# The eight normalizations of a two-layer graph network, written out without loops

## The reference, cut to what matters

```
xn = layernorm(x);  x = x + gnn(xn) + mix(xn)          # plain; inside gnn: twice with gain, shift, SiLU;
x  = x + ffn(layernorm(x))                             #        inside mix: once with gain
xn = layernorm(x);  x = x + gnn1(xn) + mix1(xn);  x = x + ffn1(layernorm(x))

layernorm(x):   (x - mean) / sqrt(var + 1e-5)
in gnn:         silu((h - mu) * rsqrt(var + eps) * g + beta)
in mix:         (out - mu) * rsqrt(var + eps) * gamma
```

## Time and profile before

| | us |
|---|---|
| time, median of 3 runs | 5152.3 (5151.81 to 5155.04) |
| the profiled execution's own time | 5157.04 |
| its span in the trace | 5155.4 |
| VectorE busy | 2133.2 (41% of the span) |
| TensorE busy | 3029.4 (59%) |
| the eight normalizations together, first `bn_stats` to last operation | 295.3 |

### The profile page before, as it was taken

One profiled execution on the slowest core, in us unless ns is written; L12 is line 12 of the kernel. 1 busy time (PEld: TensorE's weight loads), 2 busy tenths in 40 slices (PEclk: granted clock), 3 DMA queues, 4 the chain that ended last, 5 costly groups with the idle time before them and its releaser, 6 DMA issues. The chain is left out here.

```text
span 5155.4 us, 68063 instructions
## 1 busy us (share of the span) xinstructions
PE 3029.4 (59%) x14014; PEld 2154.1 (42%) x14015; DVE 2133.2 (41%) x6351; ACT 719.7 (14%) x1795; POOL 1074.6 (21%) x1216
## 2 busy tenths in 40 slices
PE   0577769949949226999287331111000288885998
PEld 0244448838837225777243130000000166663555
DVE  6899940030041640000312543333003888884333
ACT  0011110020022102322011000000000122322222
POOL 1400000000010121000300687777773000000000
PEclk6799989979979658999688665555555688987999
DMA  2511124424410012111234458888664177771000
GB/s 79 201 76 77 75 90 127 127 63 128 127 35 0 0 45 77 49 61 65 61 128 128 149 177 280 280 285 287 220 214 113 39 197 196 195 198 43 13 12 25
DMA packets 487415, 611.30 MB, mean 119 GB/s; under 512 B 78538, under 2 KB 420699, under 8 KB 483643
## 3 DMA queue, kind: packets, MB, share of 16 engines
q1 hardware_dynamic: 372268, 408.37, 25.6%
q0 software_dynamic: 48608, 139.33, 9.0%
q10 hardware_dynamic: 66480, 62.95, 4.3%
HBM read 397.38 MB, written 213.10 MB: 118 GB/s over the span
## 5 line engine op out<-in xcount | busy, mean ns | idle before, releaser
L1850 POOL DMA_INDIRECT srcs_got<-relation_rows,table_row x784 | 802.9, 1024 | 318.6 <-issue 202.2
L2372 PE MATMUL msg_acc<-msg_msg,msg_oh 128*128 128x264 f32 x1666 | 457.4, 439 | 62.8 <-DVE msg_msg L2326 62.5
L477 PE MATMUL counts_acc<-onehot_lo,onehot_key 128*128 128x400 bf16 x1962 | 376.7, 350 | 147.5 <-DVE onehot_lo L459 147.5
L459 DVE TENSOR_SCALAR onehot_lo<-node_ids,source_lo 128x800 bf16<-128x800 int16 x981 | 416.5, 425 | 0.0
L2372 PEld LDWEIGHTS msg_acc<-msg_msg,msg_oh 128*128 128x128 f32 x1666 | 328.1, 211 | 184.0 <-DVE msg_msg L2326 131.6
L1909 PE MATMUL sco_pg<-near_parts,sco_oh 128*128 x1280 | 77.5, 185 | 506.6 <-DVE sco_oh L1928 505.0
L2326 DVE TENSOR_TENSOR msg_msg<-msg_row,scores 128x256 f32<-128x256 f32 x833 | 350.2, 420 | 6.7 <-DMA msg_row<-edge_rows 4.6
L477 PEld LDWEIGHTS counts_acc<-onehot_lo,onehot_key 128*128 128x128 bf16 x1962 | 191.7, 102 | 330.2 <-DVE onehot_lo L459 187.4
L655 PE MATMUL agg_agg<-x_gnn,agg_slab 128*128 128x257 f32 x1250 | 278.0, 382 | 66.9 <-DMA agg_slab<-edge_counts 66.9
L655 PE MATMUL agg_agg<-xn,agg_slab 128*128 128x257 f32 x1250 | 277.2, 381 | 22.9 <-DMA agg_slab<-edge_counts 22.9
L655 PEld LDWEIGHTS agg_agg<-x_gnn,agg_slab 128*128 128x128 f32 x1250 | 238.2, 191 | 102.9 <-DMA agg_slab<-edge_counts 67.3
(11 more groups left out here) (406 smaller groups left out, 4273.5 us busy)
## 6 DMA issues: line engine op xcount, KB each, us to landing
msg_row<-edge_rows SPq DMA_DIRECT2D x833, 128.0 KB, 2.3
edge_rows<-srcs_got SPq DMA_DIRECT2D x112, 927.5 KB, 5.3
agg_slab<-edge_counts SPq DMA_DIRECT2D x50, 1600.0 KB, 8.2
sco_key<-target_keys ACTq DMA_DIRECT2D x256, 160.0 KB
edge_counts<-counts_out SPq DMA_DIRECT2D x100, 400.0 KB, 2.4
relation_rows<-tab_out SPq DMA_DIRECT2D x25, 1060.0 KB, 3.9
wide_w<-L_ffn_W ACTq DMA_DIRECT2D x14, 1024.0 KB, 6.8
srcs_got<-relation_rows,table_row POOLq DMA_INDIRECT x784
```

The source lines that it names most:

```text
L459: ins = nc.vector.tensor_scalar(oh_lo[:, k, j, :], c.nodes[:, 0:LO], lo[:, ds(at + j, 1)], None, ALU.is_equal)
L477: mm = nc.tensor.matmul(acc[:, k, h, 0:HALF_LO], oh_key[:, k, j, :], oh_lo[:, k, j, h * HALF_LO:(h + 1) * HALF_LO], start=False, stop=Fals ...
L1850: nc.gpsimd.indirect_dma_start(got[:, b, j, :], None, rows_of, bass.IndirectOffsetOnAxis(ap=c.row[:, at:at + 1], axis=0)).then_inc(landed[ ...
L2372: nc.tensor.matmul(acc[:, k, 0:D + HD], oh[:, j, :], msg[:, j, :], start=False, stop=False, skip_group_check=True).then_inc(used, 1)
```

## The change

`statistics` and `normalize` become one function with one block, and all its loops are written out:

- the 25 `bn_stats` are 25 instructions; the two sums that don't depend on each other (mean, variance halves) are issued without a wait between them, and the halving of the mean is moved behind the operation that ScalarE's square root waits for;
- plain: VectorE computes `moved` = -mean * rstd (128x25), then 14 tiles as before; the other 11 tiles (ACT_TILES) are ScalarE's, as Identity(x * rstd + moved) with two operands of one value per partition;
- gain: two `scalar_tensor_tensor` per tile in place of three (or two) operations. The first of tile i, (x - mean) * gain into `y`, is issued ahead of the second of tile i - 1, y * rstd + shift. `y` and `z` have four buffers each;
- gain alone (`mixn`): the second operation is y * rstd + residual, written to the residual by VectorE; GpSimd isn't used there. In `gn1` GpSimd still adds.

The diff, cut to its core:

```diff
-def statistics(g, name, src, mean, rstd):
...
-                with v.Fori(0, NT) as i:
-                    nc.vector.bn_stats(st[:, ds(i, 1), :].rearrange("p a s -> p (a s)"),
-                                       tile_of(src, i)).then_inc(loop, 1)
+def normalize(g, name, c, src, dst, gain=None, shift=None, silu=False, add_to=None):
+    deep = 4
...
+        by_act = NT - ACT_TILES if gain is None else NT
+                for i in range(NT):
+                    nc.vector.bn_stats(st[:, i, :], at(src, i)).then_inc(loop, 1)
                 v.wait_ge(loop, NT)
                 link = chain(v, link_s, 0)
+                nc.vector.tensor_tensor(t[:, 2, :], s[2], s[5], ALU.add).then_inc(half, 1)
+                nc.vector.tensor_tensor(mean, s[1], s[4], ALU.add).then_inc(half, 1)
...
+                nc.vector.tensor_scalar(t[:, 1, :], t[:, 2, :], 1.0 / D, EPS, ALU.mult, ALU.add).then_inc(var_s, 1)
+                link(nc.vector.tensor_scalar(mean, mean, 0.5, None, ALU.mult))
                 v.wait_ge(root_s, 1)
+                link(nc.vector.reciprocal(rstd, t[:, 0, :]))
+                if gain is None:
+                    nc.vector.scalar_tensor_tensor(out=moved, in0=mean, scalar=-1.0, in1=rstd,
+                                                   op0=ALU.mult, op1=ALU.mult).then_inc(ready, 1)
+                    for i in range(by_act):
+                        nc.vector.tensor_scalar(at(dst, i), at(src, i), mean[:, i:i + 1], rstd[:, i:i + 1],
+                                                ALU.subtract, ALU.mult).then_inc(last, 1)
+                    return
+                def scale(i):
+                    v.wait_ge(half, i + 3)
+                    if shift is not None:
+                        nc.vector.scalar_tensor_tensor(out=y[:, i % deep, :], in0=y[:, i % deep, :],
+                                                       scalar=rstd[:, i:i + 1], in1=shift,
+                                                       op0=ALU.mult, op1=ALU.add).then_inc(ready, 1)
+                    else:
+                        nc.vector.scalar_tensor_tensor(out=at(add_to, i), in0=y[:, i % deep, :],
+                                                       scalar=rstd[:, i:i + 1], in1=at(add_to, i),
+                                                       op0=ALU.mult, op1=ALU.add).then_inc(ready, 1)
+                for i in range(NT):
+                    if i >= deep:
+                        v.wait_ge(done if silu else ready, i - deep + 1)
+                    nc.vector.scalar_tensor_tensor(out=y[:, i % deep, :], in0=at(src, i), scalar=mean[:, i:i + 1],
+                                                   in1=gain, op0=ALU.subtract, op1=ALU.mult).then_inc(half, 1)
+                    if i:
+                        scale(i - 1)
+                scale(NT - 1)
             @block.scalar
             def _(act):
                 act.wait_ge(var_s, 1)
                 nc.scalar.activation(t[:, 0, :], t[:, 1, :], ACT.Sqrt).then_inc(root_s, 1)
+                if by_act < NT:
+                    act.wait_ge(ready, 1)
+                    for i in range(by_act, NT):
+                        nc.scalar.activation(at(dst, i), at(src, i), ACT.Identity, bias=moved[:, i:i + 1],
+                                             scale=rstd[:, i:i + 1]).then_inc(done, 1)
+                if silu:
+                    for i in range(NT):
                         act.wait_ge(ready, i + 1)
                         if add_to is None:
+                            nc.scalar.activation(at(dst, i), y[:, i % deep, :], ACT.Silu).then_inc(done, 1)
                         else:
+                            if i >= deep:
+                                act.wait_ge(last, i - deep + 1)
+                            nc.scalar.activation(z[:, i % deep, :], y[:, i % deep, :], ACT.Silu).then_inc(done, 1)
+            if silu and add_to is not None:
                 @block.gpsimd
                 def _(pl):
+                    for i in range(NT):
+                        pl.wait_ge(done, i + 1)
+                        nc.gpsimd.tensor_tensor(at(add_to, i), at(add_to, i), z[:, i % deep, :],
                                                 ALU.add).then_inc(last, 1)
```

More of the change, by code:

```diff
@@ L52 @@
 MSPAN = 17
+ACT_TILES = 11
 KSPAN = 5
@@ L524, in statistics, with at @@
         t = g.sb(ctx, f"{name}_tmp", [P, 3, NT])
-        loop, link_s, var_s, root_s = (g.sem(f"{name}_{x}") for x in ("stats", "chain", "var", "root"))
+        mean = g.sb(ctx, f"{name}_mean", [P, NT])
+        rstd = g.sb(ctx, f"{name}_rstd", [P, NT])
+        moved = g.sb(ctx, f"{name}_moved", [P, NT])
+        if gain is not None:
+            y = g.sb(ctx, f"{name}_y", [P, deep, D])
+        if silu and add_to is not None:
+            z = g.sb(ctx, f"{name}_z", [P, deep, D])
+        loop, link_s, var_s, root_s, ready, done, last, half = (
+            g.sem(f"{name}_{x}") for x in ("stats", "chain", "var", "root", "affine", "silu", "written", "half"))
+        def at(x, i):
+            return x[:, i, 0:D]
+        by_act = NT - ACT_TILES if gain is None else NT
         with nc.Block() as block:
@@ L534, in _ @@
                 s = [st[:, :, k] for k in range(6)]
-                link(nc.vector.tensor_tensor(t[:, 0, :], s[1], s[4], ALU.add))
-                link(nc.vector.tensor_scalar(mean, t[:, 0, :], 0.5, None, ALU.mult))
+                nc.vector.tensor_tensor(t[:, 2, :], s[2], s[5], ALU.add).then_inc(half, 1)
+                nc.vector.tensor_tensor(mean, s[1], s[4], ALU.add).then_inc(half, 1)
                 link(nc.vector.tensor_tensor(t[:, 0, :], s[1], s[4], ALU.subtract))
@@ L539, in _ @@
                                                     in1=t[:, 0, :], op0=ALU.mult, op1=ALU.mult))
-                link(nc.vector.tensor_tensor(t[:, 2, :], s[2], s[5], ALU.add))
+                v.wait_ge(half, 2)
                 link(nc.vector.tensor_tensor(t[:, 2, :], t[:, 2, :], t[:, 1, :], ALU.add))
@@ L550, in _ @@
                 nc.scalar.activation(t[:, 0, :], t[:, 1, :], ACT.Sqrt).then_inc(root_s, 1)
[L553 to L599, removed]
@@ L617, in step @@
                                                 ALU.add).then_inc(last, 1)
-                    tiles(pl, NT, step)
 def aggregate(g, name, c, counts, xn, wt, bias, h):
```

2 lines of the change are left out of this document (removed).

## The result

The changed kernel takes 5018.9 us, median of 4 runs (5016.6 to 5025.2), against 5152.1 us (5150.4 to 5155.0) before on the same chip: a ratio of 0.9743, interval 0.9726 to 0.9760. That is 133 us less. In the sessions of `after_sp_pad`, `before_sp_pad`, `three_ops` and `vector_add`, and of `vector_add_again`, `vadd_pool_pad` and `act_tiles10`, every kernel, the one before too (5662 and 5667 us), was slow by some 510 us, nearly all of it between the score stage's first gather and its end, so these times are compared only with times of the same session.

The account below looks back on a forecast made before the run. No engine bounds the whole; VectorE bounds the normalization windows, without filling them. 34 + 27.3 + 21.8 + 10.7 + 13.3 = 107 us off the profiled 5157.0 gives 5050, as a median 5045; 8-in-10 range 5028 to 5080.

Parts of the forecast that it names:

- Statistics: First part of all eight normalizations: unlooped `bn_stats`, no loop setup and a shorter chain save 4.25 us each, 34 us.
- duration less 0.08: Successive VectorE operations overlap, each starting after the previous one's duration less about 0.08 us; 0.344 us for `bn_stats`.
- Plain second parts: Second part of the five plain normalizations: 58.3 us together falls to 5 x 6.2 = 31, ScalarE ending last; gain 27.3 us.
- `gn0` and `mixn`: Their second parts fall from 42.7 and 31.1 us to 20.9 and 20.4; gains 21.8 and 10.7 us.
- gn1: Its second part falls from 50.3 to 37 us, gain 13.3; bounds 6 to 23.
- two things stay: In `gn1`, GpSimd's 7.26 us before its first addition and the mutual exclusion of GpSimd and VectorE were both expected to remain.
- The exclusion of the two engines: In `gn1`, VectorE and GpSimd share a port: 37 us with part running ahead, 44.4 with full durations.
- I put nothing, and 8 either way: Code behind the added instructions shifts, so other loops' turns may change: counted as zero, with 8 us either way.
- No overlap: Rival, 15%: each operation starts only when the one before has ended, giving 5077 us.
- Port: Rival, 10%: VectorE's back-to-back two-input operations give GpSimd the port late; `gn1` stays at 50 us, total 5058.
- Code supply: Rival, 2%: engines wait for about 425 written-out instructions; at 0.3 us of wait each, 5172 us, slower than before.
- Other loops: Rival, 7%: loops kept in other stages land badly, up to 0.23 us more per turn; a hundred turns make 5068 us.

Follow-up runs that it names:

- after_sp_pad: The changed kernel with 12 empty semaphore increments on SP in the block of the fourth plain normalization; 5532.7 us, ratio 0.9776, in a slower session.
- before_sp_pad: The kernel before the change with 48 empty semaphore increments on SP in the block of the fourth plain normalization; 5666.6 us, ratio 1.0007, slower session.
- three_ops: The changed kernel with three written-out operations per tile again in the two normalizations with gain and shift; 5554.2 us, ratio 0.9811, slower session.
- vector_add: The changed kernel with the additions of the second gained normalization on VectorE instead of GpSimd; 5532.3 us, ratio 0.9774, slower session.
- vector_add_again: The same kernel as `vector_add`, run again in another slower session; 5532.6 us, ratio 0.9760.
- vadd_pool_pad: The kernel of `vector_add` with 26 empty semaphore increments on GpSimd in place of its 25 additions and configuration; 5532.5 us, ratio 0.9763, slower session.
- act_tiles10: The changed kernel with 10 in place of 11 plain tiles on ScalarE, nothing else; 5531.8 us, ratio 0.9765, slower session.
- pool_loop: The changed kernel with GpSimd's additions in a loop of 6 turns of 4 again; 5028.2 us beside 5017.5 for the changed kernel, ratio 0.9760.

## Why the prediction was wrong in size

Point by point, against its own terms:

- **Statistics.** 34 us were put, of them 31.6 in the windows and 2.4 ahead of them; the windows' first parts lost 34.9. The rule "duration less 0.08" was right; the duration was not. Looped, `bn_stats` took 0.427; straight it takes mostly 0.41, and steps by (8.27 - 0.41) / 24 = 0.327 where 0.344 was put. That is 3.3 us.
- **Plain second parts.** 27.3 put, 27.8 found: each lasts 6.08 (6.2), ScalarE last by 1.03 us, its step 0.49 (0.50), its duration 0.59 (0.60). The step of `tensor_scalar` is 0.32.
- **`gn0` and `mixn`.** 21.8 and 10.7 put, 22.0 and 10.8 found; `scalar_tensor_tensor` takes 0.48 and steps by 0.396. One table load per stage, as expected.
- **`gn1`.** The step "two things stay" failed for its first thing. GpSimd's start-up was carried over at 7.26 us, but it belongs to the configuration instruction, and where that stands in the instruction list was not asked. `pool_loop` puts it back and gives 36.3 us where 37 had been worked out with it on the path; without it the second part takes 32.3. That is 4.8 us of gain not foreseen, 4.0 of them by `pool_loop`. The exclusion of the two engines was right, though not with full durations: that had been put at 44.4 us, and `pool_loop` has 36.3. And `vector_add`, without the exclusion, is faster in its window with more work on VectorE.
- **Outside the windows.** "I put nothing, and 8 either way" is the term that failed most: 19.6 us were found where 2.4 were put. 9 to 10 are the message stage, whose bound is SP's issuing: the seven meetings of the engines that the change takes out ahead of it moved SP's loops. The prediction knew from the earlier trace rows that place matters to a loop, and looked for it only on VectorE; it did not ask which stage is bound by an engine that does nothing but loop and issue. There 833 issues and 48 steps from turn to turn make 10 us of small differences. The rest is partly spread between executions, partly unexplained: the run-maxima stage is 3 to 7 us shorter, and edge counting 3 to 4 in all four traces of the changed kernel (564.8 and 564.9 us before, 560.9 to 561.5 after). For edge counting the place of the code cannot be the whole answer: `before_sp_pad`, whose edit stands behind it, has 561.4 too.

Together: 3.3 + 4.8 + 0.9 in the windows and 17.2 outside are the 26 us missed.

Of the rivals, none came. No overlap: excluded by 0.327 and 0.396. The Trainium skill, "VectorE: DVE Perf Modes", section "The DRAIN you can't avoid", has the next operation wait until the pipe is empty, but the same paragraph ends by saying that a next operation that is not held starts earlier, which the prediction left out; the trace agrees with the exception, a `bn_stats` of 0.41 us is followed after 0.33. Port: `gn1` took 32.3. Code supply: no gap without a releaser stands in the written-out stretches. Other loops: they did land differently, and better. Its opposite sign had no case of its own, which is why the low end was too high: the 8 us either way had been sized on loops of VectorE.

The range's width would have held the 9 us in the windows (5045 less 9 is 5036). It did not hold what came outside them, the message stage above all.

## What to carry to other kernels

Straight code gains three times: the loop's own turn, the overlap of neighbours, and what then comes to stand ahead of a wait (a table load, a GpSimd configuration); look for the third by asking where in the list the instruction will stand, and what runs beside it. An edit that adds or removes instructions also moves every loop behind it on the same engine; before such a change, find the stages whose length is that of one queue's own issuing, because there a tenth of a microsecond per turn is paid in full and may come back with either sign. And judge a local edit by its window first: two edits here won 6.1 us in theirs and the kernel lost 11.

## What the runs showed of the hardware

- GpSimd's first operation after its configuration started 7.2 us later (1433.7 to 1440.88 in `pool_loop`). Where the configuration stood 11.9 us ahead, the first addition started 0.09 us after its SiLU, so this time can pass beside other work. The Trainium skill, "GPSIMD Engine Reference", section "Instruction dispatch", gives about 6 us for the first call of a freshly loaded kernel; the measured 7.2 is longer.
- The gap behind the branch of one and the same outer loop on SP was 0.104, 0.119, 0.217 or 0.227 us by what stood ahead of it, and on ScalarE 0.11 or 0.19. A turn of VectorE's loop of two `tensor_scalar` took 0.82 or 1.06 us.
- An empty semaphore increment ahead of each of SP's issues cost 0.088 us per issue.
- GpSimd's median gather took 0.957 to 0.960 us in the programs where VectorE did `gn1`'s additions, and 0.946 to 0.949 in the others.
- VectorE's 0.47 us operation with two inputs takes 0.94 beside a running addition of GpSimd, and one engine doing all of it was quicker by 0.13 us per tile.
